# Where the statistics of six layer norms are finished: from VectorE to GpSimd, in a one-core kernel of two transformer-like blocks

## The chip, the core and the metric

The kernel runs on one core of a Trainium2 chip. The metric is the device time of one execution in microseconds (us); the time before is the median of three runs. TensorE (PE), VectorE (DVE), ScalarE (ACT) and GpSimd (POOL) each work through a queue of their own in order, and semaphores tie them together. SyncE (SP) issues most of the DMAs.

## What is computed

The input is 32 sequences of 256 tokens of 128 floats. Two blocks follow each other, each with two modulated sub-layers. Every sub-layer starts from a layer norm without weights:

```python
def _layernorm(x, axis=-1, eps=1e-05):
    m = jnp.mean(x, axis=axis, keepdims=True)
    v = jnp.var(x, axis=axis, keepdims=True)
    return (x - m) / jnp.sqrt(v + eps)

# block 0
h = _layernorm(x) * (1 + ca) + sa
x = x + ga * L0_attn(h)        # RWKV time mixing; inside: layer_norm ln1 of h, layer_norm ln2 of h + its output
h = _layernorm(x) * (1 + cb) + sb
x = x + gb * L0_ffn(h)         # relu MLP, 128 -> 512 -> 128
# block 1
h = _layernorm(x) * (1 + ca) + sa
x = x + ga * L1_attn(h)        # 16 heads of 8, 4 key groups, rotary embedding, softmax
h = _layernorm(x) * (1 + cb) + sb
x = x + gb * L1_ffn(h)         # router, top 2 of 8 experts, 128 -> 512 -> 128
```

Four `_layernorm` and the two weighted norms in `L0_attn` make six norms per token. All arithmetic of the norms is in float32.

## The kernel before

The tokens go through in 16 chunks of 512 (two sequences). A chunk is held as four tiles of 128 tokens on the partitions by 128 features along the row (`NT = 4`), or transposed. The order of the steps on each engine is written out by hand in the table `ORDER`, one list of step names for each engine, and each engine's program walks its list. Steps whose names begin with A and E are block 0's time mixing, B its MLP and the projections of block 1, C and G block 1's attention scores and softmax, R the last norm and the router, S the sort of tokens to experts, M and W the experts, K the gather and sum at the end. Chunks overlap: at any moment the queues hold steps of several chunks in turn.

A norm is done by three engines. It happens in six places per chunk, so 96 times:

- VectorE's `stats` (steps `A_ln0s`, `A_ln1s`, `E_ln2s`, `B_ln0s`, `B_ln1s`, `R_ln`): four `bn_stats` (L1291), one per tile of 128 tokens, each giving six numbers per token (for the even and for the odd elements a count, a mean and a sum of squared differences); a wait for them; four `bn_aggr` (L1294) that make mean and variance; a wait; the negated mean (L1296); the variance plus epsilon (L1297), which signals `ln_var`.
- GpSimd's `scale_bias` (steps `A_ln`, `E_ln2`, `B_ln`, `R_ln`): the power of -0.5 (L663), a wait on itself through `ln_rstd`, and the bias, -mean times that (L665). Both work on 4 numbers per partition.
- ScalarE's `norm` (L785): four activations, one per tile, with that scale and bias. Before it, ScalarE waits for `ln_rstd`.

What comes behind in a norm's chain: for `A_ln1s` and the norms of B and E, TensorE transposes the result (L1013) and ScalarE takes it out of PSUM. For `A_ln0s` and `R_ln`, VectorE multiplies by the modulation (L1433, L1627) and GpSimd adds (L701, L744). GpSimd also forms the token differences (L708, L715), gates and adds a residual (L720, L725), splits off bfloat16 parts (L735), and issues the scatters (L756) and gathers (L775) of the expert stage.

Of the kernel before, what the change touches and what calls it, by code (L numbers as in the profile page):

```python
# [12 lines left out]
ALU = mybir.AluOpType  # L13
# [3 lines left out]
P = 128  # L17
D = 128
# [3 lines left out]
NT = N // P  # L22
# [8 lines left out]
EPS = 1e-5  # L31
# [49 lines left out]

EVENTS = """
p_ld p_ldw p_ldx p_st p_vec p_scl p_pol p_mm
ln_var ln_rstd
a_ld0 a_ld1 a_ldm a_ldg a_z0 a_h0 a_h a_norm a_tp a_xn
e_dx e_xr e_xk e_xv e_r e_th e_k e_v e_ky e_m e_exp e_dv e_att e_wo e_x1 e_norm e_tp e_xn
e_fk e_rl e_sq e_fr e_th2 e_vk e_aq e_y e_ga e_out
# [34 lines left out]
def order_of(engine, names):  # L122

    return {k: n + 1 for n, k in enumerate(k for k in steps(engine) if k[0] in names)}
# [41 lines left out]
def program(nc, a):  # L166
    ctx = ExitStack()
    with ctx:
        def sb(name, shape, dt=F32):
            return ctx.enter_context(nc.sbuf_tensor(name, shape, dt))  # L170
# [13 lines left out]
        ln_var, ln_rstd = order_of("DVE", LN_STATS), order_of("Pool", LN_RSTD)  # L184
# [15 lines left out]
        col = sb("col", [P, NCOL])  # L200
        negw = sb("negw", [P, 1])
        half = sb("half", [P, NT])
        wk, wv, wr, wo = (sb(n, [P, D]) for n in ("wk", "wv", "wr", "wo"))
        fwk = sb("fwk", [P, FC * P])
        fwr = sb("fwr", [P, D])
# [31 lines left out]
        ax = sb("ax", [P, 2, NT, D])  # L237
        am = sb("am", [P, BC, 2, D])
        ag = sb("ag", [P, BC, D])
        ast = sb("ast", [P, NT, 6])  # L240
        amv = sb("amv", [P, NT, 2])
        avar = sb("avar", [P, 2, NT])
        ars = sb("ars", [P, 2, NT])
        az = sb("az", [P, NT, D])
        ah = sb("ah", [P, NT, D])
# [13 lines left out]
        aE = aE[:, 0, :, :]  # L259
        ax1 = sb("ax1", [P, NT, D])  # L260
        est = sb("est", [P, NT, 6])
        emv = sb("emv", [P, NT, 2])
        evar = sb("evar", [P, 2, NT])
        ers = sb("ers", [P, 2, NT])
        ez = sb("ez", [P, NT, D])
        ath2 = sb("ath2", [P, N])
# [7 lines left out]
        bx = sb("bx", [P, 2, NT, D])  # L274
        bm = sb("bm", [P, BC, D])
        bst = sb("bst", [P, NT, 6])
        bmv = sb("bmv", [P, NT, 2])
        bvar = sb("bvar", [P, 2, NT])
        brs = sb("brs", [P, 2, NT])
        bz = sb("bz", [P, NT, D])  # L280
        bh = sb("bh", [P, N])
# [1 line left out]
        bx2 = sb("bx2", [P, NT, D])  # L283
# [25 lines left out]
        cxo = sb("cxo", [P, NT, D])  # L309

        rm = sb("rm", [P, BC, 2, D])
        rst = sb("rst", [P, NT, 6])
        rmv = sb("rmv", [P, NT, 2])
        rvar = sb("rvar", [P, 2, NT])
        rrs = sb("rrs", [P, 2, NT])
        rz = sb("rz", [P, NT, D])
        rhn = sb("rhn", [P, NT, D])
# [31 lines left out]
        S = {n: ctx.enter_context(nc.semaphore(n)) for n in EVENTS}  # L349
# [30 lines left out]
        def k_set(c):  # L380

            return k_sets[c], k_sets[:c + 1].count(k_sets[c])
# [44 lines left out]
        with nc.Block() as block:  # L427
# [228 lines left out]

            @block.gpsimd
            def _(pool):
                def scale_bias(s, i, stat, var, rs):

                    n = ln_rstd[s, i]
                    pool.wait_ge(S["ln_var"], ln_var[stat])
                    pool.tensor_tensor(rs[:, 0, :], var[:, 0, :], half[:, :], ALU.pow).then_inc(S["ln_rstd"], 1)  # L663
                    pool.wait_ge(S["ln_rstd"], 2 * n - 1)
                    pool.tensor_tensor(rs[:, 1, :], var[:, 1, :], rs[:, 0, :], ALU.mult).then_inc(S["ln_rstd"], 1)  # L665

                before_ = indirect_before()

# [12 lines left out]
                for s, i in steps("Pool"):  # L681
                    if s == "I_set":
                        pool.memset(half[:, :], -0.5)
                        pool.memset(onesf[:, :], 1.0)
                        pool.memset(sone[:, :], 1.0)
                        pool.memset(axn[:, :, 0:1], 0.0)
                        pool.memset(aE[:, :, 0:1], NEG_INIT)
                        pool.memset(aAB[:, :, :, 0:1].rearrange("p a b o -> p (a b) o"), 0.0)
                        pool.memset(mH[:, :], 0.0)
                        pool.memset(bva[:, :, :, :, :].rearrange("p s t g v -> p (s t g v)"), 0.0  # L690
                                    ).then_inc(S["p_pol"], 1)
                        pool.wait_ge(S["p_pol"], 1)
                        pool.memset(bva[:, :, :, :, 8:9].rearrange("p s t g v -> p (s t g) v"), 1.0
                                    ).then_inc(S["p_pol"], 1)
                    if s == "A_ln":
                        scale_bias(s, i, (("A_ln0s", "A_ln1s")[i % 2], i // 2), avar, ars)
                    if s == "A_h":
                        pool.wait_ge(S["a_h0"], i + 1)
                        if i:
# [8 lines left out]
                        pool.tensor_tensor(adx[:, :, :], axn[:, :, 1:T + 1], axn[:, :, 0:T],  # L708
                                           ALU.subtract).then_inc(S["e_dx"], 1)
                    if s == "E_ln2":  # L710
                        scale_bias(s, i, ("E_ln2s", i), evar, ers)
                    if s == "E_dx2":
                        pool.wait_ge(S["e_xn"], i + 1)
                        pool.wait_ge(S["e_xv"], i + 1)
# [11 lines left out]
                                           ALU.add).then_inc(S["e_out"], 1)  # L726

                    if s == "B_ln":
                        scale_bias(s, i, (("B_ln0s", "B_ln1s")[i % 2], i // 2), bvar, brs)
                    if s == "B_sub":  # L730
                        c, k = divmod(i, PARTS - 1)
                        pool.wait_ge(S["b_p"], PARTS * c + k + 1)
# [2 lines left out]
                        pool.tensor_tensor(bqk, bqk, bp[:, k, :], ALU.subtract).then_inc(S["b_r"], 1)  # L735

                    if s == "R_ln":
                        scale_bias(s, i, ("R_ln", i), rvar, rrs)
                    if s == "R_hn":
                        pool.wait_ge(S["r_h0"], i + 1)  # L740
                        if i:
# [18 lines left out]
                    if s == "K_g":  # L760
                        c, k = divmod(i, 2)
                        z, n = k_set(c)
# [523 lines left out]
            def _(dve):  # L1286
                v = Count(dve, S["vec"])

                def stats(src_, st, mv, var):
                    for t in range(NT):  # L1290
                        v(dve.bn_stats(st[:, t, :], src_[:, t, :]))  # L1291
                    v.wait()
                    for t in range(NT):
                        v(dve.bn_aggr(mv[:, t, :], st[:, t, :]))  # L1294
                    v.wait()
                    dve.tensor_scalar(var[:, 1, :], mv[:, :, 0], -1.0, None, ALU.mult)  # L1296
                    dve.tensor_scalar(var[:, 0, :], mv[:, :, 1], EPS, None, ALU.add).then_inc(S["ln_var"], 1)  # L1297

                def mix(out_, m_):
                    return dve.scalar_tensor_tensor(out_[:, :, :], adx[:, :, :], col[:, m_:m_ + 1],  # L1300
# [28 lines left out]
                for s, i in steps("DVE"):  # L1329
# [9 lines left out]
                    if s == "I_rows":  # L1339

                        rb = rowbuf[i]
                        for j in (SA, CA, SB, CB, GA, GB):
                            dve.wait_ge(S["p_mm"], 2 * i + 1 + j // 3)
                            src_ = bank[MOD[2 * i + j // 3]][0:B, (j % 3) * D:(j % 3 + 1) * D]
# [5 lines left out]
                            else:  # L1350
# [6 lines left out]
                                ins = dve.scalar_tensor_tensor(out_, rowsgn[:, z], -1.0, rowneg[:, z], ALU.add, ALU.mult)  # L1357
# [4 lines left out]
                    if s == "I_col":  # L1362
                        dve.wait_ge(S["p_mm"], M_COL)
                        for j in range(MODC):
                            ins = dve.tensor_scalar(colbuf[:, :, j], bank[SETUP][:, j * B:(j + 1) * B],
                                                    0.0 if j % 2 else 1.0, None, ALU.add)
# [57 lines left out]
                    if s == "A_ln0s":  # L1424
                        dve.wait_ge(S[f"a_ld{i % 2}"], 16 * (i // 2 + 1))
                        if i:

                            dve.wait_ge(S["a_norm"], i)
                        stats(ax[:, i % 2, :, :], ast, amv, avar)
                    if s == "A_c":  # L1430
                        dve.wait_ge(S["a_z0"], i + 1)
                        dve.wait_ge(S["a_ldm"], 16 * (i + 1))
# [1 line left out]
                                          per_batch(am[:, :, CA, :], az), ALU.mult).then_inc(S["a_h0"], 1)  # L1434
                    if s == "A_ln1s":
                        dve.wait_ge(S["a_h"], i + 1)
                        stats(ah, ast, amv, avar)

                    if s == "E_mix":
                        dve.wait_ge(S["e_dx"], 2 * i + 1)  # L1440
# [62 lines left out]
                    if s == "E_ln2s":  # L1503
                        dve.wait_ge(S["e_x1"], i + 1)
                        if i:
                            dve.wait_ge(S["e_norm"], i)
                        stats(ax1, est, emv, evar)
                    if s == "E_mix2":
                        dve.wait_ge(S["e_dx"], 2 * i + 2)
                        dve.wait_ge(S["e_r"], i + 1)  # L1510
# [13 lines left out]
                    if s == "B_ln0s":  # L1524
                        dve.wait_ge(S["e_out"], i + 1)
                        if i:
                            dve.wait_ge(S["b_norm"], 2 * i)
                        stats(bx[:, i % 2, :, :], bst, bmv, bvar)
                    if s == "B_x2":
                        dve.wait_ge(S["b_w2"], 2 * i + 2)  # L1530
                        dve.wait_ge(S["b_ldm"], 16 * (i + 1))
# [6 lines left out]
                                          ALU.add).then_inc(S["b_x2"], 1)  # L1538
                    if s == "B_ln1s":
                        dve.wait_ge(S["b_x2"], i + 1)  # L1540
                        stats(bx2, bst, bmv, bvar)
                    if s == "B_q":
                        c, j = divmod(i, 2)
                        b_, tab = ((col[:, BQ:BQ + 1], cos), (bqr[:, 0:1], sin))[j]
# [52 lines left out]
                    if s == "G_o":  # L1597
# [7 lines left out]
                        for j in range(2):  # L1605
                            ins = dve.tensor_tensor(cctx[:, 2 * b:2 * b + 2, :, pp, j, :], t_[:, j, :, :, 0:HD],
                                                    crs[:, 2 * j:2 * j + 2, :].unsqueeze(3)
                                                    .broadcast_to([P, 2, KV, HD]), ALU.mult)
# [11 lines left out]

                    if s == "R_ln":
                        dve.wait_ge(S["c_y"], i + 1)
                        stats(cxo, rst, rmv, rvar)
                    if s == "R_c":
                        dve.wait_ge(S["r_z0"], i + 1)
                        dve.wait_ge(S["r_ldm"], 16 * (i + 1))
# [90 lines left out]
                    if s == "K_sum":  # L1717
                        k, n = k_set(i)
# [5 lines left out]
                        for t in range(NT):  # L1724
                            ins = dve.scalar_tensor_tensor(g_[:, 0, t, :], g_[:, 1, t, :], w_[:, t, P2:P2 + 1],
                                                           g_[:, 0, t, :], ALU.mult, ALU.add)
                        ins.then_inc(S["k_sum"], 1)
                    if s == "K_out":
                        k, n = k_set(i)
# [296 lines left out]
```

## Time and profile before

| | us |
|---|---|
| median of three runs | 1633.04 |
| lowest and highest | 1629.73, 1641.36 |
| span of the profiled execution, first to last instruction | 1622.0 |

The profiled execution's own time is not listed apart from its span. The span is 11.0 us under the median and 7.7 us under the fastest run; what lies outside it is the start and end of the program. The span is cut below into a start up to 200 us, a middle from 200 to 1290 us in which all kinds of steps overlap, and an end in which experts and gathers are left. Shares of busy time are averages over stages, and matmul ends are modelled.

### The profile page before, as it was taken

To read this page: it belongs to the slowest core of one execution; us is meant where nothing else is said; L and a number is where in the kernel's file an instruction comes from. 1 tells how busy PE (TensorE), PEld (TensorE's weight loads), DVE (VectorE), ACT (ScalarE), POOL (GpSimd) and SP (SyncE) were. 2 spreads that over 40 slices of the span, in tenths; PEclk is the share of its full clock that TensorE was granted. 3 is DMA by queue.
4 is the path that set the end of the run, shared out by engine and by line. 5 is a ranking of instruction groups with operands and counts; after the bars stand their busy time and mean duration, and the time that the engine had idled before them with its cause. 6 is when DMAs were issued, how large, how long until landed. Compare 5 with 4: busy or idle time off the path is not lost.

```text
span 1622.0 us, 26719 instructions
## 1 busy us (share of the span) xinstructions
PE 1353.9 (83%) x8354; PEld 866.5 (53%) x8354; DVE 1095.2 (68%) x2943; ACT 990.8 (61%) x2295; POOL 545.8 (34%) x589
## 2 busy tenths in 40 slices
PE   3466897889888888999999979899899998998681
PEld 1234454534445444666666644467566754687571
DVE  5568879788989898676876895967755754140113
ACT  1354765667676556877777766567568565555430
POOL 2123222313122475212112256435322134344335
PEclk7677998989999889999999998799999999999885
DMA  4012135142321424454544524256555556788772
GB/s 126 7 36 72 42 114 167 46 132 64 110 77 30 121 83 116 139 157 124 168 134 141 154 87 137 78 164 193 159 169 171 159 166 207 225 275 276 225 244 76
DMA packets 202037, 217.68 MB, mean 134 GB/s; under 512 B 17419, under 2 KB 167526, under 8 KB 199593
## 3 DMA queue, kind: packets, MB, share of 16 engines
q1 hardware_dynamic: 193704, 199.18, 41.0%
q0 software_dynamic: 8192, 16.79, 3.4%
q8 instruction: 68, 1.11, 0.3%
q14 instruction: 73, 0.59, 0.1%
HBM read 161.18 MB, written 53.94 MB: 133 GB/s over the span
## 4 chain that ended last, share of the span: by engine, by line
PE 43%; DVE 21%; issue 11%; ACT 8%; POOL 7%; DMA 6%; SPq 2%; POOLq 0%; ACTq 0%; another core or an unknown queue 0%; DVEq 0%
DVE cmx L1581 6%; PE bank L1228 5%; PE bank L1045 5%; PE bank L1028 5%; PE bank L1212 5%; PE bank L1196 4%; PE bank L1151 3%; PE bank L1124 2%; POOL kg L775 2%; DMA kg<-y_slots,sslot 2%; PE bank L1164 2%; PE bank L1013 2%; POOL bhs L775 2%; ACT wide L903 2%; PE bank L1140 2%
## 5 line engine op out<-in xcount | busy, mean ns | idle before, releaser
L1581 DVE TENSOR_REDUCE cmx<-bank 128x2 f32<-128x512 f32 x512 | 328.7, 684 | 97.4 <-PE bank L1196 89.3
L903 ACT ACTIVATE wide<-bank 128x512 f32<-128x512 f32 x512 | 280.0, 609 | 69.2 <-PE bank L1212 64.6
L1212 PE MATMUL bank<-wide 75*128 75x512 bf16 x512 | 174.9, 407 | 23.2 <-DVE cmx L1581 14.7
L1196 PE MATMUL bank<-wide 72*128 72x256 bf16 x1024 | 176.2, 283 | 20.6 <-DVE cmx L1581 15.6
L756 POOL DMA_INDIRECT x_slots<-sx,sslot x128 | 128.1, 1001 | 111.3 <-issue 46.9
L1196 PEld LDWEIGHTS bank<-wide 72*128 72x128 bf16 x1024 | 92.0, 101 | 124.7 <-issue 48.2
L1228 PE MATMUL bank<-wide,bva 128*32 128x512 f32 x1024 | 146.5, 646 | 9.9 <-ACT wide L903 5.7
L942 ACT ACTIVATE mH<-bank,mW 128x128 f32<-128x128 f32 x376 | 107.0, 371 | 57.8 <-PE bank L1028 50.9
L1028 PE MATMUL bank<-mT,mW 128*128 128x128 f32 x872 | 123.8, 287 | 17.0 <-DMA mW<-in_wexp 7.9
L1028 PEld LDWEIGHTS bank<-mT,mW 128*128 128x128 f32 x872 | 112.6, 199 | 36.3 <-issue 14.7
L775 POOL DMA_INDIRECT kg<-y_slots,sslot x88 | 85.9, 976 | 117.9 <-DMA kg<-y_slots,sslot 35.6
L1212 PEld LDWEIGHTS bank<-wide 75*128 75x128 bf16 x512 | 49.3, 104 | 131.1 <-ACT wide L903 60.1
L1045 PE MATMUL bank<-mW,mH 128*128 128x128 f32 x752 | 109.8, 289 | 0.0
L663 POOL TENSOR_TENSOR brs<-bvar,half 128x4 f32<-128x4 f32 x32 | 33.9, 1058 | 218.2 <-DVE bvar L1297 218.1
L1045 PEld LDWEIGHTS bank<-mW,mH 128*128 128x128 f32 x752 | 91.8, 192 | 6.3
L1151 PE MATMUL bank<-bh,w 128*128 128x512 f32 x128 | 81.2, 720 | 15.1 <-ACT bhs L879 8.0
L735 POOL TENSOR_TENSOR bqk<-bqk,bp 128x768 f32<-128x768 f32 x32 | 54.9, 1715 | 88.9 <-ACT bp L889 88.8
L879 ACT ACTIVATE bhs<-bank,col 128x512 f32<-128x512 f32 x64 | 44.0, 687 | 57.7 <-PE bank L1151 53.4
L949 ACT ACTIVATE mX<-bank 128x128 f32<-128x128 f32 x120 | 33.5, 279 | 73.3 <-PE bank L1045 66.1
L1124 PE MATMUL bank<-axk,fwk 128*128 128x512 f32 x128 | 70.2, 650 | 5.5 <-DVE axk L1300 5.3
L1603 DVE RECIPROCAL crs<-bank 128x16 f32<-128x16 f32 x64 | 16.2, 253 | 84.0 <-PE bank L1234 80.6
L1722 DVE TENSOR_SCALAR kg<-kg,rinfo 128x128 f32<-128x128 f32 x44 | 9.8, 285 | 91.9 <-DMA kg<-y_slots,sslot 91.8
(296 smaller groups left out, 2863.4 us busy)
## 6 DMA issues: line engine op xcount, KB each, us to landing
mW<-in_wexp SPq DMA_DIRECT2D x109, 514.0 KB
wide<-q_parts SPq DMA_DIRECT2D x32, 576.0 KB
inner<-in_wexp SPq DMA_DIRECT2D x31, 514.0 KB
wide<-in_wexp SPq DMA_DIRECT2D x16, 514.0 KB
mX<-x_slots SPq DMA_DIRECT2D x27, 256.0 KB
y_slots<-mX SPq DMA_DIRECT2D x27, 256.0 KB
q_parts<-bp SPq DMA_DIRECT2D x32, 192.0 KB
x_slots<-mH SPq DMA_DIRECT2D x2, 3072.0 KB, 10.9
```

The source lines that it names most:

```text
L756: pool.indirect_dma_start(out=x_slots[GROUP_OF[c]], out_offset=bass.IndirectOffsetOnAxis(ap=sslot[:, c, k, t:t + 1], axis=0), in_=sx[:, c ...
L775: pool.indirect_dma_start(out=kg[z][:, k, t, :], out_offset=None, in_=y_slots[GROUP_OF[c]], in_offset=bass.IndirectOffsetOnAxis(ap=sslot[: ...
L903: act.activation(cP[:, i % 8, :], bank[seat["G_s", i]][:, :], ACT.Exp, scale=SCALE).then_inc(S["c_p"], 1)
L942: act.activation(hidden[z][:, c * P:(c + 1) * P], bank[seat[k]][:, c * P:(c + 1) * P], ACT.Relu, bias=w_[:, FC * P + c:FC * P + c + 1]).th ...
L1028: ins = pe.matmul(ps[:, c * P:(c + 1) * P], weights[w_][:, c * P:(c + 1) * P], mT[:, q % 2, j * P:(j + 1) * P], start=True, stop=True)
L1045: ins = pe.matmul(ps[:, 0:P], hidden[z][:, c * P:(c + 1) * P], weights[w_slot(i)[0]][:, o:o + D], start=False, stop=(c == FC - 1))
L1124: pe.matmul(ps[:, :], fwk[:, j * P:(j + 1) * P], flat(axk[:, :, :]), start=True, stop=True).then_inc(S["e_fk"], 1)
L1151: pe.matmul(ps[:, :], w1[:, j * P:(j + 1) * P], bh[:, :], start=True, stop=True).then_inc(S["b_w1"], 1)
L1196: ins = pe.matmul(ps[:, j * T:(j + 1) * T], cQ[0:SROWS, z, h, tt * P:(tt + 1) * P], cK[0:SROWS, z, h // G, :], start=True, stop=True)
L1212: pe.matmul(ps[:, :], cK[0:KROWS, z, g, sc_ * P:(sc_ + 1) * P], cQ[0:KROWS, z, h0:h0 + 2, :], start=True, stop=True).then_inc(S["c_s2"], 1)
L1228: ins = pe.matmul(CO[32 * g:32 * g + 32, :], bva[:, c % 2, b * 2 + sc_, g, :], cP[:, (4 * i + g) % 8, :], start=(sc_ == 0), stop=(sc_ == 1))
L1581: dve.tensor_reduce(cmx[:, u % 2, tt, 2 * hp:2 * hp + 2], bank[seat["C_s", i]][:, :].rearrange("p (j t) -> p j t", j=2), AX_X, ALU.max, ne ...
```

## The change

On VectorE the four `bn_aggr` and the two small operations go, with the two waits between them; the last `bn_stats` signals `ln_var` itself. On GpSimd `scale_bias` reads the six raw numbers per token and forms everything: it scales them (L666 of the new file), takes the difference and the sums of the even and odd halves, squares the difference, adds epsilon, adds the parts of the variance, and then does the same power and product as before. Six operations are new, five waits on its own new counter `ln_own`, and a wait that its previous norm is done, since the scratch tiles `lst`, `lsum`, `ldif`, `lsq`, `lvar` are shared by all six norms. Two `memset` make the table of scales. The tables `ORDER` are the same, so no step changes its place on any engine.

```diff
@@ I_set, set-up on GpSimd @@
+                        pool.memset(lscale[:, :], 1.0 / D)
...
                         pool.wait_ge(S["p_pol"], 1)
+                        pool.memset(lscale[:, 1:6:3], -0.5)
@@ GpSimd @@
-                def scale_bias(s, i, stat, var, rs):
+                ln = Count(pool, S["ln_own"])
+
+                def scale_bias(s, i, stat, st, rs):
 
                     n = ln_rstd[s, i]
+                    even, odd = lst[:, :, 1:3], lst[:, :, 4:6]
                     pool.wait_ge(S["ln_var"], ln_var[stat])
-                    pool.tensor_tensor(rs[:, 0, :], var[:, 0, :], half[:, :], ALU.pow).then_inc(S["ln_rstd"], 1)
+                    if n > 1:
+                        pool.wait_ge(S["ln_rstd"], 2 * n - 2)
+                    else:
+                        pool.wait_ge(S["p_pol"], 2)
+                    ln(pool.tensor_tensor(lst[:, :, :], st[:, :, :], lscale[:, :].unsqueeze(1).broadcast_to([P, NT, 6]),
+                                          ALU.mult))
+                    ln.wait()
+                    ln(pool.tensor_tensor(ldif[:, :], even[:, :, 0], odd[:, :, 0], ALU.subtract))
+                    ln(pool.tensor_tensor(lsum[:, :, :], even, odd, ALU.add))
+                    ln.wait(ln.n - 1)
+                    ln(pool.tensor_tensor(lsq[:, :], ldif[:, :], ldif[:, :], ALU.mult))
+                    ln.wait()
+                    ln(pool.tensor_scalar(lsq[:, :], lsq[:, :], EPS, None, ALU.add))
+                    ln.wait()
+                    ln(pool.tensor_tensor(lvar[:, :], lsum[:, :, 1], lsq[:, :], ALU.add))
+                    ln.wait()
+                    pool.tensor_tensor(rs[:, 0, :], lvar[:, :], half[:, :], ALU.pow).then_inc(S["ln_rstd"], 1)
                     pool.wait_ge(S["ln_rstd"], 2 * n - 1)
-                    pool.tensor_tensor(rs[:, 1, :], var[:, 1, :], rs[:, 0, :], ALU.mult).then_inc(S["ln_rstd"], 1)
+                    pool.tensor_tensor(rs[:, 1, :], lsum[:, :, 0], rs[:, 0, :], ALU.mult).then_inc(S["ln_rstd"], 1)
@@ VectorE @@
-                def stats(src_, st, mv, var):
+                def stats(src_, st):
                     for t in range(NT):
-                        v(dve.bn_stats(st[:, t, :], src_[:, t, :]))
-                    v.wait()
-                    for t in range(NT):
-                        v(dve.bn_aggr(mv[:, t, :], st[:, t, :]))
-                    v.wait()
-                    dve.tensor_scalar(var[:, 1, :], mv[:, :, 0], -1.0, None, ALU.mult)
-                    dve.tensor_scalar(var[:, 0, :], mv[:, :, 1], EPS, None, ALU.add).then_inc(S["ln_var"], 1)
+                        ins = dve.bn_stats(st[:, t, :], src_[:, t, :])
+                    ins.then_inc(S["ln_var"], 1)
```

The callers pass the tiles of raw statistics (`ast`, `est`, `bst`, `rst`) instead of those of variances, which are gone.

## Rows read from the trace of the kernel before

**Rows 1.** The page: busy time of the engines, and the chain that ended last.

```profile
PE 1353.9 (83%) x8354; PEld 866.5 (53%) x8354; DVE 1095.2 (68%) x2943; ACT 990.8 (61%) x2295; POOL 545.8 (34%) x589
PE 43%; DVE 21%; issue 11%; ACT 8%; POOL 7%; DMA 6%; SPq 2%; POOLq 0%; ACTq 0%; another core or an unknown queue 0%; DVEq 0%
```

**Rows 2.** Busy time by stretches (start:end, length, then each engine's busy time).

```profile
200.00:450.00 250.00, 215.53 (x1207) 113.11 (x1206) 213.93 (x566) 164.86 (x321) 62.32 (x69) 0.92 0.33 103
450.00:700.00 250.00, 217.81 (x1278) 125.44 (x1276) 213.62 (x552) 164.86 (x341) 103.21 (x107) 0.92 0.34 98
```

**Rows 3.** The timeline (start, length, in us) of one norm of B.

```profile
430.27 0.86 DVE L1291 BATCH_NORM_STATS2 bst<-bx 128x6 f32<-128x128 f32 x4
431.17 0.38 DVE L1294 BATCH_NORM_AGGREGATE bmv<-bst 128x2 f32<-128x6 f32 x4
...
431.58 0.17 DVE L1296 TENSOR_SCALAR bvar<-bmv 128x4 f32<-128x4 f32 x1
431.66 0.16 DVE L1297 TENSOR_SCALAR bvar<-bmv 128x4 f32<-128x4 f32 x1
431.73 0.68 DVE L1501 TENSOR_TENSOR ax<-ah,bank 128x512 f32<-128x512 f32 x1
431.90 1.01 POOL L663 TENSOR_TENSOR brs<-bvar,half 128x4 f32<-128x4 f32 x1 [24.64 <-DVE bvar L1297]
...
432.99 0.20 POOL L665 TENSOR_TENSOR brs<-bvar,brs 128x4 f32<-128x4 f32 x1
```

**Rows 4.** GpSimd's groups by line and form (xcount, busy us, mean ns).

```profile
L663 POOL TENSOR_TENSOR brs<-bvar,half 128x4 f32<-128x4 f32 x32 | 33.9, 1058 | 218.2 <-DVE bvar L1297 218.1
L708 POOL TENSOR_TENSOR adx<-axn 128x512 f32<-128x512 f32 x16 | 16.9, 1055 | 54.4 <-ACT axn L822 54.4
L665 POOL TENSOR_TENSOR brs<-bvar,brs 128x4 f32<-128x4 f32 x32 | 6.9, 214 | 2.5
L683 POOL MEMSET half<- 128x4 f32 x1 | 0.1, 101 | 0.3 <-POOLq L2012 0.3
```

**Rows 5.** L665 and L663 alone: ns min/median/max.

```profile
L665 POOL TENSOR_TENSOR brs<-bvar,brs x32: 198/199/686, 85.8 to 1272.1; 128x4 f32<-128x4 f32 x32
L663 POOL TENSOR_TENSOR brs<-bvar,half x32: 1006/1017/1439, 84.7 to 1271.0; 128x4 f32<-128x4 f32 x32
```

**Rows 6.** The chain that ended last, 213 to 222 us (start, length): a norm of E, then one of B.

```profile
214.96 0.88 DVE est L1291 x4
...
216.35 0.16 DVE evar L1297
216.52 0.60 DVE bz L1534
...
219.03 0.79 DVE bst L1291 x4
...
220.44 0.08 DVE bvar L1297
220.51 0.07 issue
220.58 1.02 POOL brs L663
```

**Rows 7.** Waits of ScalarE for GpSimd's results (us in total, times, longest).

```profile
ACT ez L785 <- POOL ers L665: 37.3, 6, 16.5
ACT az L785 <- POOL ars L665: 22.7, 5, 14.9
ACT rz L785 <- POOL rrs L665: 7.7, 8, 2.2
ACT bz L785 <- POOL brs L665: 6.9, 6, 3.6
```

**Rows 8.** The timeline where L708 of GpSimd and L1619 of VectorE meet.

```profile
447.11 1.04 POOL L708 TENSOR_TENSOR adx<-axn 128x512 f32<-128x512 f32 x1 [4.19 <-ACT axn L822]
...
447.25 1.45 DVE L1619 TENSOR_TENSOR cxo<-cx,cos_ 128x512 f32<-128x512 f32 x1
```

**Rows 9.** L1619 alone: ns min/median/max.

```profile
L1619 DVE TENSOR_TENSOR cxo<-cx,cos_ x16: 691/693/1446, 245.0 to 1421.5; 128x512 f32<-128x512 f32 x16
```

**Rows 10.** L663 alone by stretches (start:end, length, busy, count, clock, DMA).

```profile
200.00:1290.00 1090.00, 79.81 (x77) 0.95 0.42 125
1290.00:1622.00 332.00, 2.08 (x2) 0.88 0.69 212
```

More of the change, by code:

```diff
@@ L83 @@
 p_ld p_ldw p_ldx p_st p_vec p_scl p_pol p_mm
-ln_var ln_rstd
+ln_var ln_own ln_rstd
 a_ld0 a_ld1 a_ldm a_ldg a_z0 a_h0 a_h a_norm a_tp a_xn
@@ L202, in program @@
         half = sb("half", [P, NT])
+        lscale = sb("lscale", [P, 6])
+        lst = sb("lst", [P, NT, 6])
+        lsum = sb("lsum", [P, NT, 2])
+        ldif, lsq, lvar = (sb(n, [P, NT]) for n in ("ldif", "lsq", "lvar"))
         wk, wv, wr, wo = (sb(n, [P, D]) for n in ("wk", "wv", "wr", "wo"))
@@ L240, in program @@
         ast = sb("ast", [P, NT, 6])
-        amv = sb("amv", [P, NT, 2])
-        avar = sb("avar", [P, 2, NT])
         ars = sb("ars", [P, 2, NT])
@@ L261, in program @@
         est = sb("est", [P, NT, 6])
-        emv = sb("emv", [P, NT, 2])
-        evar = sb("evar", [P, 2, NT])
         ers = sb("ers", [P, 2, NT])
@@ L276, in program @@
         bst = sb("bst", [P, NT, 6])
-        bmv = sb("bmv", [P, NT, 2])
-        bvar = sb("bvar", [P, 2, NT])
         brs = sb("brs", [P, 2, NT])
@@ L312, in program @@
         rst = sb("rst", [P, NT, 6])
-        rmv = sb("rmv", [P, NT, 2])
-        rvar = sb("rvar", [P, 2, NT])
         rrs = sb("rrs", [P, 2, NT])
@@ L695, in _ @@
                     if s == "A_ln":
-                        scale_bias(s, i, (("A_ln0s", "A_ln1s")[i % 2], i // 2), avar, ars)
+                        scale_bias(s, i, (("A_ln0s", "A_ln1s")[i % 2], i // 2), ast, ars)
                     if s == "A_h":
@@ L710, in _ @@
                     if s == "E_ln2":
-                        scale_bias(s, i, ("E_ln2s", i), evar, ers)
+                        scale_bias(s, i, ("E_ln2s", i), est, ers)
                     if s == "E_dx2":
@@ L728, in _ @@
                     if s == "B_ln":
-                        scale_bias(s, i, (("B_ln0s", "B_ln1s")[i % 2], i // 2), bvar, brs)
+                        scale_bias(s, i, (("B_ln0s", "B_ln1s")[i % 2], i // 2), bst, brs)
                     if s == "B_sub":
@@ L737, in _ @@
                     if s == "R_ln":
-                        scale_bias(s, i, ("R_ln", i), rvar, rrs)
+                        scale_bias(s, i, ("R_ln", i), rst, rrs)
                     if s == "R_hn":
@@ L1428, in _ @@
                             dve.wait_ge(S["a_norm"], i)
-                        stats(ax[:, i % 2, :, :], ast, amv, avar)
+                        stats(ax[:, i % 2, :, :], ast)
                     if s == "A_c":
@@ L1436, in _ @@
                         dve.wait_ge(S["a_h"], i + 1)
-                        stats(ah, ast, amv, avar)
+                        stats(ah, ast)
                     if s == "E_mix":
@@ L1506, in _ @@
                             dve.wait_ge(S["e_norm"], i)
-                        stats(ax1, est, emv, evar)
+                        stats(ax1, est)
                     if s == "E_mix2":
@@ L1527, in _ @@
                             dve.wait_ge(S["b_norm"], 2 * i)
-                        stats(bx[:, i % 2, :, :], bst, bmv, bvar)
+                        stats(bx[:, i % 2, :, :], bst)
                     if s == "B_x2":
@@ L1540, in _ @@
                         dve.wait_ge(S["b_x2"], i + 1)
-                        stats(bx2, bst, bmv, bvar)
+                        stats(bx2, bst)
                     if s == "B_q":
@@ L1622, in _ @@
                         dve.wait_ge(S["c_y"], i + 1)
-                        stats(cxo, rst, rmv, rvar)
+                        stats(cxo, rst)
                     if s == "R_c":
```

## The prediction

> **What bounds the kernel now.** The page comes first, for the engines' load and the make-up of the chain that ended last [rows 1]: TensorE is busy 83% of the span and VectorE 68%, and the chain is TensorE's for 43% and VectorE's for 21%. GpSimd is busy 34% and holds 7% of it. No engine alone sets the end. The busy time by stretches is next [rows 2]: from 200 to 700 us TensorE works 433 of 500 us and VectorE 428. There the two are level, so in that stretch a microsecond taken off VectorE can be worth something. The chain in order of time then tells where the norms stand on it [rows 6]. I went through it in stretches of 50 us and counted. The `bn_stats` of 30 of the 96 norms lie on it. Behind 11 of these the chain goes on to GpSimd's L663, as in the second norm of the rows; behind the other 19 it goes on with VectorE's next instruction, as in the first. Three more norms have only their GpSimd part on the chain, because GpSimd came to them late. The first kind pays for a longer norm, the second is paid for a shorter VectorE step. The change does both at once, so the time hangs on the balance.
>
> **VectorE gets shorter.** In the timeline of one norm [rows 3] the `bn_stats` end at 430.27 + 0.86 = 431.13 us and VectorE's next instruction starts at 431.73. These 0.60 us (four `bn_aggr`, two small operations and the waits) go: 96 x 0.60 = 58 us of VectorE's time, 5% of its 1095. They count on the path only where the chain stays on VectorE: 19 x 0.60 = 11.4 us.
>
> **GpSimd gets longer.** Six operations are new. The nearest row is L665, a product of 4 numbers per partition: 198 ns at least [rows 5]. Four of the new ones are two-input operations on 4 or 8 numbers; I take 0.20 us each. The scaling of 24 numbers gets a slope: L708 takes 1055 ns for 512 [rows 4], so (1055 - 198) / 508 = 1.7 ns for each, and 198 + 20 x 1.7 = 0.23 us. The addition of epsilon is a `tensor_scalar`, which GpSimd has nowhere before. Its bounds are 0.10 us (the `memset` of 4 numbers) [rows 4] and 0.20; I take 0.20, since it reads as L665 does. The sum is 1.23 us. Between dependent operations there is the semaphore: L663 ends at 432.91 and L665 starts at 432.99 [rows 3], 0.08 us. Five new waits less the one that waits for the last but one (the addition in between covers it) make 4 x 0.08 = 0.32 us. At last the hold-ups: L665's mean is 214 ns against its least of 198, and L663's 1058 against 1006 [rows 4, 5], 16 to 52 ns for each operation, say 25; six of them make 0.15 us. GpSimd is thus longer by 1.23 + 0.32 + 0.15 = 1.7 us a norm, between 1.4 (with epsilon at 0.10 and no hold-up) and 1.9 (hold-ups of 52 ns). Over 96 norms this is 163 us, and GpSimd goes from 546 to about 690 us busy (the gaps don't count as busy), 43% of the span.
>
> **What a norm's result loses.** Before, from the end of `bn_stats` to the start of L663 it is 431.90 - 431.13 = 0.77 us [rows 3]. After, it is 0.08 us for the signal (as from the end of L1297, 431.82, to 431.90) and 1.7. The result comes 0.08 + 1.7 - 0.77 = 1.0 us later (0.7 to 1.2). Where GpSimd was late itself, the whole 1.7 counts.
>
> **The sum on the chain of before.** 11 x 1.0 + 3 x 1.7 - 19 x 0.60 = 11.0 + 5.1 - 11.4 = +4.7 us.
>
> **What that sum leaves out.** The chain is one path, and others run beside it with little slack. Delays off the chain can become the path, and savings on it end where another path takes over; both push upward. ScalarE stands still for GpSimd's result before 6 + 5 + 8 + 6 = 25 norms [rows 7]. That many results are awaited at once, 11 to 14 of them on the chain. The other 11 or so delay ScalarE by 1.0 us each with every product behind in its queue. ScalarE is busy 61% and makes up some of it; I count a third, +3.7 us. The opposite correction, VectorE's savings elsewhere, needs VectorE to be on the path, which the chain has counted. So the forecast is +4.7 + 3.7 = +8.4 us, on the span 1622.0 + 8.4 = 1630.4. What lies outside the span is untouched but for two `memset` of 0.1 us [rows 4] long before the first norm. The median stands 11.0 us above the span: 1633.0 + 8.4 = 1641.4. No transfer is touched. GpSimd's queue delays whatever is behind a norm by 1.7 us: L701, L715, L708, L744, and in the middle the scatters L756 and gathers L775; GpSimd's own idle time, two thirds of the span, hides nearly all of this. After 1290 us only two norms are left [rows 10] and the change is worth at most 2 x 1.7 us there. VectorE gets no new wait: the tile of raw numbers is free again by the waits that held for ScalarE's normed tile.
>
> **Row against rule: the port.** VectorE's L1619, with both inputs in SBUF, takes 693 ns as a rule and 1446 once [rows 9]; that once it starts at 447.25 while L708 of GpSimd runs from 447.11 to 448.15, and ends 0.55 us behind it, as if it had started late [rows 8]. So one engine holds up the other, and each new GpSimd operation is one more chance in both directions. By its longest case a small operation waits 686 - 198 = 0.49 us [rows 5]. The Trainium skill says this in "SBUF — State Buffer", "Who interferes with whom": a VectorE instruction with two SBUF inputs and a GpSimd instruction that reads SBUF exclude each other, and the later one waits in full; by it, breaking the work into six short reads gives VectorE six gaps to slip into. The rival that this makes is the third below.
>
> **The rivals.**
> *VectorE's relief wins* (chance 0.15). In 200 to 700 us VectorE is as loaded as TensorE. If GpSimd's longer part is hidden in most places and all 30 norms whose `bn_stats` are on the chain give their 0.60 us, it is -18.0 us: span 1604.0, median 1615.0. For it speak the level loads; against it, that behind 11 of the 30 the chain goes straight to GpSimd.
> *The norm's latency wins, on ScalarE's queue* (chance 0.24, slower). All 25 awaited results delay what follows by 1.0 us and the three late ones by 1.7: 25 + 5.1 = 30.1, less half of VectorE's gain (5.7), +24.4 us: 1657.4. It needs the delayed activations of L785 to be followed on TensorE's queue by transposes (L1013) that nothing can overtake, since the queues are in order. From about 16 net delays of 1.0 us it passes 1%. Against it: ScalarE's idle 39% and the fact that only 11 norms go through on the chain.
> *The port* (chance 0.09, slower). Each of the 14 norms whose GpSimd part is on the chain loses two of its gaps to a VectorE operation and waits 0.49 us in each: 14 x 0.98 = +13.7 on top of +8.4, 1655.1. Against it: L665's median is 199, its least 198.
> *It does nothing* (in the middle case). Losses and gains cancel, 1633; that is only 8 us from the forecast.
>
> **How the numbers follow.** The forecast's case, from 0 to +16 us, has 0.52. The two slower rivals have 0.33 and the faster one 0.15. A difference of 1%, 16 us, is about what the measurement of this kernel can tell from none. Faster by over 1% (under 1616.7) is half in, half out of the first rival's reach, so 0.12; slower by over 1% (over 1649.4) takes the slower rivals nearly whole, 0.30; the rest is 0.58. The range leaves out one in ten at either side: from 1619 (most of the faster rival) to 1661 (the latency rival with its delays at 1.2 us instead of 1.0, 1657.4 + 5).
>
> **What would show it.** VectorE's busy time falls by some 60 us and it goes straight from `bn_stats` to its next work. GpSimd rises by 120 to 165 us. From the end of `bn_stats` to GpSimd's power operation it is 1.8 us instead of 0.77. ScalarE's waits for GpSimd number more than 25 and come to over 75 + 25 us. If the time falls instead, the chain of waits should hold fewer VectorE pieces and no more GpSimd. I am wrong if the new operations take much more than 0.2 us, or if VectorE, not TensorE and the latencies, sets the pace from 200 to 700 us.

## The result and the profile after

The changed kernel takes 1679.3 us (median of 4 runs, 1678.9 to 1688.0) against 1631.4 for the kernel before (4 runs): ratio 1.0288, 95% interval 1.0249 to 1.0326. That is +47 us, 2.9% slower. The forecast was +8 us and its range ended at 1661. The profiled execution's span went from 1622.0 to 1677.5 us, +55.5. That is more than 47 because the profiled execution of the kernel before was shorter than the timed ones: in every execution with both numbers listed the time is only about 2 us above the span of its core (1679.3 against 1677.5 in the changed kernel). The 11.0 us between median and span in the table above are thus for the most part the spread between executions, not the start and end of the program.

The page of the changed kernel, busy time and chain, answers to [rows 1]:

```profile
PE 1374.9 (82%) x8354; PEld 874.9 (52%) x8354; DVE 1034.1 (62%) x2367; ACT 994.5 (59%) x2295; POOL 676.4 (40%) x1167
PE 34%; POOL 20%; issue 16%; DVE 14%; ACT 7%; DMA 6%; another core or an unknown queue 1%; SPq 1%; POOLq 0%; ACTq 0%; DVEq 0%
```

VectorE's busy time fell by 61 us and GpSimd's rose by 131, as worked out. (The prediction's own terms give 678 us for GpSimd, not the 690 it states; 676.4 were measured.) But GpSimd's share of the chain went from 7% to 20% while VectorE's fell from 21% to 14%. I went through the chain again and counted power operations on it: 14 before, 56 after (21 of B, 13 of A, 12 of R, 10 of E).

The same place in the program as [rows 3], in the timeline of the changed kernel:

```profile
451.40 0.86 DVE L1308 BATCH_NORM_STATS2 bst<-bx 128x6 f32<-128x128 f32 x4
452.34 0.23 POOL L666 TENSOR_TENSOR lst<-bst,lscale 128x24 f32<-128x24 f32 x1 [24.56 <-DVE bst L1308]
452.65 0.20 POOL L669 TENSOR_TENSOR ldif<-lst 128x4 f32<-128x4 f32 x1
...
452.81 0.20 POOL L670 TENSOR_TENSOR lsum<-lst 128x8 f32<-128x8 f32 x1
452.96 0.20 POOL L672 TENSOR_TENSOR lsq<-ldif 128x4 f32<-128x4 f32 x1
453.25 0.23 POOL L674 TENSOR_SCALAR lsq<-lsq 128x4 f32<-128x4 f32 x1
453.51 0.87 DVE L1308 BATCH_NORM_STATS2 est<-ax 128x6 f32<-128x128 f32 x4
453.56 0.20 POOL L676 TENSOR_TENSOR lvar<-lsum,lsq 128x4 f32<-128x4 f32 x1
453.85 1.04 POOL L678 TENSOR_TENSOR brs<-lvar,half 128x4 f32<-128x4 f32 x1
...
454.96 0.20 POOL L680 TENSOR_TENSOR brs<-lsum,brs 128x4 f32<-128x4 f32 x1
...
455.31 0.23 POOL L666 TENSOR_TENSOR lst<-est,lscale 128x24 f32<-128x24 f32 x1
...
457.93 0.20 POOL L680 TENSOR_TENSOR ers<-lsum,ers 128x4 f32<-128x4 f32 x1
```

The six new operations take 453.85 - 452.34 = 1.51 us. For the norm of B the result comes 2.90 us behind the end of `bn_stats` (452.26 to 455.16); before it was 2.06 (431.13 to 433.19, [rows 3]). That is +0.84 and is the best case. The norm of E behind it shows the second effect. Its `bn_stats` end at 454.38, but GpSimd is still in the norm of B, starts at 455.31, and the result comes at 458.13: 3.75 us. Over all 96 norms, worked out from the two traces, the time from the end of `bn_stats` to the result is 2.05 us at least and 2.06 in the median before, 2.90 at least and 3.46 in the median after. The typical norm is late by 1.4 us, not by 1.0. Another norm is not the main thing in the way: 74 norms found GpSimd ready before and 46 after; of the 50 others after, 16 waited for another norm's operations and 34 for other work in GpSimd's queue, most often the addition L718 (12 times), the split L752 (9) and the scatters L773 (6).

ScalarE's waits for GpSimd's results, answering to [rows 7]:

```profile
ACT ez L802 <- POOL ers L680: 48.3, 9, 17.7
ACT az L802 <- POOL ars L680: 40.3, 15, 14.4
ACT bz L802 <- POOL brs L680: 24.8, 16, 4.8
ACT rz L802 <- POOL rrs L680: 21.9, 14, 3.8
```

The awaited norms go from 25 to 54 and the waiting from 75 to 135 us. TensorE's waits for the normed tiles show in this view of its own:

```profile
PE bank L1030 <- ACT bz L802: 28.4, 17, 7.5
PE bank L1030 <- ACT ez L802: 18.6, 8, 6.7
PE bank L1030 <- ACT az L802: 16.8, 3, 14.4
```

Before, the same three (L1013) came to 20.2, 9.7 and 13.7 us: +20 us.

The loss builds up over the whole middle, after a first step. Comparing the starts of the same instruction in both traces, the 16 `cxo` additions (L1619, now L1631) are late by 13.4 us at the first chunk, 23.1 at the fifth, 31.4 at the ninth, 45.0 at the twelfth and 48.0 at the last. The span ends 55.5 us later.

The busy time by stretches, answering to [rows 2]:

```profile
200.00:450.00 250.00, 207.82 (x1123) 108.42 (x1126) 193.88 (x417) 157.50 (x301) 81.65 (x175) 0.88 0.33 102
450.00:700.00 250.00, 214.32 (x1192) 116.38 (x1185) 196.91 (x435) 161.84 (x326) 127.30 (x234) 0.89 0.30 85
```

VectorE's relief shows (428 to 391 us) and nothing takes its place: TensorE works less too in these stretches, and its granted clock (as a share of full speed, a mean over each stretch) went from 0.92 to 0.88 and 0.89.

### The profile page after: what moved, and what is told of

Same layout as the page of the kernel before. It is cut to its first block, busy times and chain, and to the rows that moved or that the text cites. A ratio compares the mean times of both kernels' runs of the same rounds, so it can differ in the third digit from the quotient of the medians.

```text
span 1677.5 us, 26817 instructions
## 1 busy us (share of the span) xinstructions
PE 1374.9 (82%) x8354; PEld 874.9 (52%) x8354; DVE 1034.1 (62%) x2367; ACT 994.5 (59%) x2295; POOL 676.4 (40%) x1167
## 4 chain that ended last, share of the span: by engine, by line
PE 34%; POOL 20%; issue 16%; DVE 14%; ACT 7%; DMA 6%; another core or an unknown queue 1%; SPq 1%; POOLq 0%; ACTq 0%; DVEq 0%
POOL x_slots L773 4%; PE bank L1062 4%; PE bank L1245 4%; PE bank L1045 4%; DVE cmx L1593 3%; PE bank L1229 3%; PE bank L1213 3%; PE bank L1168 3%; POOL kg L792 2%; PE bank L1141 2%; DMA kg<-y_slots,sslot 2%; POOL bhs L792 2%; PE bank L1181 2%; DMA x_slots<-sx,sslot 1%; PE bank L1030 1%
## 5 line engine op out<-in xcount | busy, mean ns | idle before, releaser
L1593 DVE TENSOR_REDUCE cmx<-bank 128x2 f32<-128x512 f32 x512 | 329.2, 684 | 133.4 <-PE bank L1213 126.0
L773 POOL DMA_INDIRECT x_slots<-sx,sslot x128 | 129.8, 1014 | 107.1 <-issue 42.4
L1245 PE MATMUL bank<-wide,bva 128*32 128x512 f32 x1024 | 153.2, 674 | 9.5 <-ACT wide L920 6.1
L752 POOL TENSOR_TENSOR bqk<-bqk,bp 128x768 f32<-128x768 f32 x32 | 54.7, 1710 | 85.1 <-ACT bp L906 85.1
L666 POOL TENSOR_TENSOR lst<-bst,lscale 128x24 f32<-128x24 f32 x32 | 8.3, 258 | 191.7 <-DVE bst L1308 191.4
```

Source lines behind the costliest of these rows:

```text
L773: pool.indirect_dma_start(out=x_slots[GROUP_OF[c]], out_offset=bass.IndirectOffsetOnAxis(ap=sslot[:, c, k, t:t + 1], axis=0), in_=sx[:, c ...
L1245: ins = pe.matmul(CO[32 * g:32 * g + 32, :], bva[:, c % 2, b * 2 + sc_, g, :], cP[:, (4 * i + g) % 8, :], start=(sc_ == 0), stop=(sc_ == 1))
L1593: dve.tensor_reduce(cmx[:, u % 2, tt, 2 * hp:2 * hp + 2], bank[seat["C_s", i]][:, :].rearrange("p (j t) -> p j t", j=2), AX_X, ALU.max, ne ...
```

## The experiments

Each kernel was timed against the kernel before, on the same chip. The cuts of code are shortened. "Late" is counted from the end of `bn_stats` to the end of the bias product, at its least over the 96 norms, unless a median is named.

**Does a later result cost, or a longer queue?** Two kernels put the same six kinds of operations on GpSimd, on scratch tiles, once behind and once ahead of a norm's result. VectorE's part is that of before.

```diff
                     pool.wait_ge(S["ln_var"], ln_var[stat])
+                    six(); ln.wait()          # "ahead" only
                     pool.tensor_tensor(rs[:, 0, :], var[:, 0, :], half[:, :], ALU.pow)...
                     pool.tensor_tensor(rs[:, 1, :], var[:, 1, :], rs[:, 0, :], ALU.mult)...
+                    six()                     # "behind" only
```

> The kernel before, with six operations of the new kinds put on GpSimd behind each norm's result (behind L665), on scratch tiles; VectorE's part is as before. GpSimd is some 1.5 us longer per norm, but the norm's own result comes when it did. If the loss is the later result (latency theory), this costs little: 0 to +15 us. If the loss is that GpSimd's queue is free later for what stands behind the norm (occupancy theory), it costs as much as the change or more, +45 to +60 us, since VectorE gives nothing back here.

Measured: ratio 1.0085 (1.0041 to 1.0129), +14 us.

> The kernel before, with the same six operations on scratch tiles put ahead of the power operation, behind the wait for the variances. Result and queue are both 1.5 us later; VectorE's part is as before. Latency theory: as 57 norms have their GpSimd part on the chain of the changed kernel, 57 x 1.5 = 85 us, so +70 to +95 us. Occupancy theory: the same as with the six operations behind the result, within 10 us.

Measured: 1.0408 (1.0334 to 1.0482), +67 us. The occupancy of GpSimd's queue is a real but small part; the later result is worth 67 - 14 = 53 us for 1.5 us (39 to 67, worked out from the two intervals), or 35 us for each microsecond by which all 96 results are late. The latency theory holds in kind, though the 67 is just under its range of 70 to 95; the occupancy theory explains only the 14. That part was more than the nothing I had given it: work behind a norm, such as another norm's, starts later; in the mean over the 96 norms even the results of this kernel are 0.4 us late (2.72 to 3.13 us). The number of norms on the chain is no price: it is 52 with the six operations ahead, fewer than the 56 of the changed kernel (57 in the expectation), and 36 with them behind.

**Is it proportional?** Three of the operations ahead of the result, instead of six.

```diff
+                    three(); ln.wait()        # product, difference, sum
```

> The kernel before, with three operations (0.6 us, two waits among and behind them) ahead of the power operation instead of six. If the cost of a later result rises in proportion, the 3.2% that six cost by latency for 1.5 us give 1.3 to 1.7% for 0.7 us, and the queue 0.4%: +28 us in all. If there is slack that the first few tenths of a microsecond use up, it is under +12 us.

Measured: 1.0170 (1.0110 to 1.0229), +28 us. Its results are 0.74 us late, half of the 1.5. That fits a proportion, within a wide interval (18 to 37 us), and rules out slack that would have kept it under 12 us. Nothing shorter was tested alone.

**And towards earlier?** The power operation of before replaced by a product of constants, which makes the scale of every norm a constant.

```diff
-pool.tensor_tensor(rs[:, 0, :], var[:, 0, :], half[:, :], ALU.pow)
+pool.tensor_tensor(rs[:, 0, :], half[:, :], half[:, :], ALU.mult)
```

> The kernel before with the power operation (1.0 us) replaced by a product of constants (0.2 us): the scale of each norm is then a constant and does not depend on its variance. The result comes 0.8 us earlier in all 96 norms. If a norm's time counts by its place on the chain of the kernel before, it gives 14 x 0.8 = -11 us. If it is worth in this direction what it costs in the other (53 us for 1.5 us later), it gives -28 us.

Measured: 1.0042 (1.0009 to 1.0075), +7 us. In its trace the operation takes 198 ns:

```profile
L663 POOL TENSOR_TENSOR ars<-half x32: 193/198/217, 9.2 to 1095.6; 128x4 f32<-128x4 f32 x32
```

So 0.8 us earlier gives nothing; both expectations, -11 and -28 us, are wrong. The chain of before had 14 x 0.8 = 11 us of this operation's time on it, and taking them away brought none of them. The time bends near the point where the kernel before stands: 0.74 us later costs, 0.8 us earlier brings nothing. That it is longer at all goes with the clock: these ten executions ran at a mean granted clock of 0.900, the twenty of the kernel before beside them at 0.905. Over the 58 executions of the kernel before in the experiments the time is about 10 us longer for each 0.01 of clock less, so 0.006 (0.8996 against 0.9054) would make 6 us. Why the clock was lower is open; the kernel also computes other numbers.

**Which norms?** The change for 48 norms at a time.

```diff
 if s == "A_ln" or s == "E_ln2": scale_bias(...)      # new, raw numbers; VectorE's part likewise
 if s == "B_ln" or s == "R_ln":  scale_bias_old(...)  # as before; the other kernel has it the other way round
```

> The change for the norms of A and E alone (48 of 96); those of B and R as before. Latency theory: these stand in the one serial path that goes from chunk to chunk (norm, norm, time mixing, norm), so most of the loss is here, +30 to +48 us. If loss comes from each norm alike (port or occupancy theory), it is half, about +24 us.

> The change for the norms of B and R alone (48 of 96); those of A and E as before. Latency theory: these have slack, 0 to +15 us. Theories that charge each norm alike: about +24 us.

Measured: A and E 1.0074 (1.0040 to 1.0108), +12 us; B and R 1.0130 (1.0076 to 1.0184), +21 us. I had expected the loss in A and E, as the serial path, and slack in B and R; both are wrong. It is in both, and if anything more in B and R, so no one serial path carries it. The 24 us each of a loss that charges every norm alike fit B and R, and are too much for A and E (7 to 18 us). The halves sum to 2.0% where the whole costs 2.9%. A likely reason, not shown, is that both together also get into each other's way on GpSimd, as the norm of E did above.

**The port.** Six memsets, which read nothing from SBUF, in place of the six reading operations ahead of the result.

```diff
+ln(pool.memset(dum[:, 0, :], 0.0)); ln.wait()     # six times, with the waits of before
```

> The kernel before, with six memsets of 128 numbers (208 ns each) ahead of the power operation, with the same waits as the six operations of before: some 1.6 us later, as there, but none of the six reads SBUF. If a good part of the +4.1% is that GpSimd's reads and VectorE's two-input operations hold each other up (port theory), this is at least 15 us cheaper than the six reading operations. If the loss is the later result alone, it is the same within 10 us: +65 to +80 us.

Measured: 1.0330 (1.0281 to 1.0380), +54 us against +67. This falls between the two expectations: the 13 us between them are more than the 10 that I had allowed for the later result alone and less than the 15 that I had set for the port theory, and the intervals overlap. About half of the 13 has another cause: the memset chain is 0.17 us shorter per norm (3.40 us at least to the result, against 3.57), which at 35 us per microsecond is 6 us. The groups by line show that hold-ups exist. The memsets:

```profile
L668 POOL MEMSET dum<- 128x128 f32 x96 | 20.0, 209 | 403.1 <-DVE bvar L1313 204.0 <-DVE rvar L1313 100.9 <-DVE evar L1313 51.7
L671 POOL MEMSET dum<- 128x128 f32 x96 | 20.0, 208 | 0.0
```

The changed kernel, one of its reading operations (ns min/median/max) and its mean:

```profile
L672 POOL TENSOR_TENSOR lsq<-ldif x96: 192/200/1170, 9.5 to 1471.8; 128x4 f32<-128x4 f32 x96
```
```profile
L672 POOL TENSOR_TENSOR lsq<-ldif 128x4 f32<-128x4 f32 x96 | 22.5, 234 | 0.0
```

A mean of 234 on a median of 200 is 34 ns of hold-up. It is the largest of the six; the six together come to 0.15 us, the prediction's figure. One of the hold-ups, in the timeline:

```profile
226.29 0.69 DVE L1549 TENSOR_TENSOR bx<-bx,bz 128x512 f32<-128x512 f32 x1
226.32 0.72 POOL L672 TENSOR_TENSOR lsq<-ldif 128x4 f32<-128x4 f32 x1
```

The small operation starts 0.03 us behind a VectorE operation with two inputs in SBUF and ends 0.06 us behind its end. The trace agrees with the Trainium skill ("SBUF — State Buffer", "Who interferes with whom") that such a VectorE operation holds up a GpSimd operation that reads SBUF; the memsets, which only write, took 335 ns at most against 1170. VectorE itself loses nothing by it: its busy time is 1092.4 us with the six reading operations ahead and 1095.2 before. The port is at most a small part.

**What VectorE's time is worth.** First, VectorE's old work kept in the changed kernel, behind its signal.

```diff
                     ins.then_inc(S["ln_var"], 1)
+                    (wait; four bn_aggr; wait; two tensor_scalar, on unused tiles; wait)
```

> The changed kernel, with VectorE's old work (four aggregations and two small operations with their waits) kept behind its signal, on unused tiles; nobody waits for their results. The difference to the changed kernel is what VectorE's 0.6 us per norm are worth. By the chain of the kernel before (19 norms whose path stays on VectorE) it is 11 us more than the change, so +58 us in all, between +50 and +70. If VectorE's time is worth nothing, it is +48 as the change.

Measured: 1.0311 (1.0270 to 1.0351), 1686.2 us. Against the changed kernel's 1.0288 VectorE's 0.6 us per norm are worth 4 us. The two intervals together leave 9 us to either side of that, so it is told neither from nothing nor from the 11 us of the expectation. Then two kernels in which the result is not late. One keeps two new operations; it leaves the squared difference of the half means and epsilon out of the variance. The other has none of the six and takes the raw numbers of the even half as they are.

```diff
 # two steps (in words)
 lst = st * lscale
-ldif, lsq = ...; lsq += EPS; lvar = lsum[1] + lsq
 lsum = even + odd
+the power works on lsum[1]
 # raw (in words)
+the power works on st[:, :, 2], the product on st[:, :, 1]
```

> The changed kernel with two new GpSimd operations per norm instead of six; it leaves out of the variance the squared difference of the two half means, and epsilon. The result then comes about when it did before (2 operations and 2 waits, 0.6 us, for VectorE's 0.6 us), GpSimd is 0.6 us longer and VectorE 0.6 us shorter per norm. Latency theory: -10 to +5 us against the kernel before, VectorE's gain less a little of GpSimd's queue. A theory in which VectorE's gain is worth nothing and the queue costs: +5 to +15 us.

> The changed kernel without any of the six new GpSimd operations; the power and the product work on the raw numbers of the even half, so scale and bias of each norm are wrong ones. VectorE is 0.6 us shorter and the result 0.7 us earlier per norm than in the kernel before. An earlier result alone gave nothing. If VectorE's time is worth something when the result is not late, this gives what the two-step kernel gave, -12 us, or more, to -25 us. If the two-step kernel was faster for another reason, 0.

Measured: 0.9925 (0.9897 to 0.9952) and 0.9926 (0.9893 to 0.9959), -12 us both. The results of the first come 0.1 us earlier at the least and 0.3 us later in the median than before, those of the second 0.7 us earlier. So VectorE's time is worth 12 us (7 to 17) as long as the results are on time, close to the 11.4 of the prediction, and a still earlier result adds nothing. Both kernels compute other numbers than the reference; TensorE and ScalarE have as many instructions as before, but whether the numbers play a part in the time was not tested. When the results are late, the measured worth is 4 us, give or take 9: less than 12 by its middle value, and not shown to be less.

**A version that computes the reference.** The aggregations stay on VectorE and only epsilon and the sign go to GpSimd.

```diff
 # VectorE: the last bn_aggr signals ln_var
+ln(pool.tensor_scalar(lvar[:, 0, :], mv[:, :, 1], EPS, None, ALU.add))
+ln(pool.tensor_scalar(lvar[:, 1, :], mv[:, :, 0], -1.0, None, ALU.mult))
+ln.wait(ln.n - 1)
 power on lvar[:, 0, :], product on lvar[:, 1, :]
```

> A version that computes what the reference does: the four aggregations stay on VectorE and signal themselves; only epsilon and the sign of the mean go to GpSimd (two operations, the second beside the first). VectorE is 0.2 us shorter, the result about as late as before (+0.05 us), GpSimd 0.3 us longer per norm. If results on time and a shorter VectorE are what pays: -4 us, between -8 and +2. If GpSimd's queue is what costs, 0 to +4 us.

Measured: 1.0028 (0.9998 to 1.0059), no gain. Its timeline tells why:

```profile
439.33 0.38 DVE L1305 BATCH_NORM_AGGREGATE bmv<-bst 128x2 f32<-128x6 f32 x4
439.80 0.23 POOL L670 TENSOR_SCALAR lvar<-bmv 128x4 f32<-128x4 f32 x1 [26.10 <-DVE bmv L1305]
440.11 0.23 POOL L671 TENSOR_SCALAR lvar<-bmv 128x4 f32<-128x4 f32 x1
440.31 1.03 POOL L673 TENSOR_TENSOR brs<-lvar,half 128x4 f32<-128x4 f32 x1
```

The second operation starts 0.31 us behind the first, not beside it, and the result is 0.34 us later than before (2.39 us at least against 2.05), where I had counted 0.05. By the prices above this would be an estimate of 0.34 x 35 = 12 us for the later result and 5 for the queue (0.5 us of the 1.5 that cost 14), less 4 for VectorE's 0.2 us, +13; measured are +5 us (0 to 10). So the price of 35 us per microsecond, found at 0.7 to 1.5 us, may be too high for a few tenths.

## Why the prediction was wrong, step by step

- *VectorE gets shorter*: right. 61 us less busy. In most norms it goes from `bn_stats` at once to its next work; in the norm above the next work (L1513) waits 0.53 us for TensorE.
- *GpSimd gets longer*, 1.7 us a norm: right in its terms. The six take 1.51 us without hold-ups against the 1.55 predicted; the scaling 0.233 against 0.23, epsilon 0.230 against 0.20; the hold-ups 0.15 as predicted.
- *What a norm's result loses*, 1.0 us: right for a norm alone (0.85 and hold-ups), too small for the typical one (1.4). I had not counted that a norm more often finds GpSimd busy, with another norm (16 of 96) or with other work that has itself moved back (34; together 22 before). The sentence that GpSimd's idle time hides nearly all of the queue's delay fails: six operations behind the result cost 14 us.
- *The sum on the chain of before*, +4.7 us: this is the step that failed. It took 14 norms as the ones that pay: 11.0 + 5.1 = 16.1 us for what the norms lose. With VectorE's old work kept, so that nothing is gained against it, the changed kernel costs +51 us (44 to 57). With results 0.9 to 1.4 us later, 56 norms have their GpSimd part on the chain. The chain of before shows one path; that many others ran beside it, shorter by less than a microsecond, is the reading that fits these numbers. The trace of before had a hint: worked out from its timeline, ScalarE began with L785 within 0.13 us of the result in 31 of the 96 norms and within 0.9 us in 51 of them. The view of waits lists only the 25 in which it stood still.
- *What that sum leaves out*, +3.7 us: the mechanism was the right one and its size far off. The measured prices are 35 us for each microsecond of lateness and 14 us for the queue. With 0.85 us, or 1.0 with hold-ups, that is 30 to 35 us and 14, together 44 to 49. Beside it stand the measured 51 us without VectorE's gain and 47 with it. Both prices have wide intervals, so the nearness is partly luck.
- *The rivals*: the one on ScalarE's queue (+24 us, chance 0.24) names the right mechanism and has half of the loss. It had only ScalarE's 25 waits. The port is real and small. The relief of VectorE exists (12 us with results on time); how much of it is left when results are late is not settled.
- *The median stands 11.0 us above the span*: the reading is wrong (it is about 2 us in one and the same execution), but it only moved the forecast from the span back to the median, so no step rests on it. The range's upper end adds up to 1662 (1657.4 + 5), not 1661; the measured time lies beyond either.

Shown by experiments: that a later result costs, 28 us at 0.74 us and 67 at 1.5, that the queue costs little, that an earlier result gives nothing, and that VectorE's time is worth 12 us with results on time. Not settled: how much of the loss is the lower clock. TensorE's 8354 matmuls took 1374.9 us instead of 1353.9 at a mean granted clock of 0.895 instead of 0.909. The four timed executions of the changed kernel have a mean clock of 0.890, the 58 of the kernel before 0.906; at the 10 us for each 0.01 found above, an estimate of 16 of the 47 us goes with the clock. Whether the lower clock makes the time longer, or the longer waits make the clock lower, is not shown. It stays open too whether VectorE's gain shrinks when results are late. Its waits for the scores' matmuls grew from 89.3 us to 126.0, but with the raw numbers, where the gain is there, they grew as well, to 115.4 (kernel before, changed kernel, raw numbers; us in total, times, longest):

```profile
DVE cmx L1581 <- PE bank L1196: 89.3, 75, 9.7
DVE cmx L1593 <- PE bank L1213: 126.0, 98, 9.7
DVE cmx L1581 <- PE bank L1201: 115.4, 96, 9.7
```

## What to carry to other kernels

Before lengthening a step that occurs a hundred times in a kernel with a fixed order on each engine, count in the timeline how soon its result is taken up at each place, not only where a wait or the chain names it: here 51 of 96 results were taken up within 0.9 us, where the chain named 14. That such a count forecasts the loss was not tested. The chain gave a far too low value for time added (16 us against 51). For time removed it was right once (VectorE's, 11.4 against 12) and wrong once (the power operation's, 11 against nothing), so the one agreement may be luck. And moving this work off the loaded engine paid only in the two kernels where the result did not come later for it.

## What the hardware showed that I had not expected

- Small GpSimd operations on 4 to 8 numbers: 0.15 us from start to start without a wait on the one before (452.81 to 452.96), 0.28 to 0.31 us in the medians with one. Two `tensor_scalar` without a wait between them were also 0.31 us apart (439.80 to 440.11).
- One reading operation of 200 ns took up to 1170 ns, while six memsets in its place had means of 205 to 209 ns and took 335 ns at most: the long delays came to operations that read SBUF. In the changed kernel 45 of the 672 small ones lasted over 0.06 us more than their median, 16 us in all.
- An 0.8 us faster power operation in all 96 norms gave +0.4% and not a gain.
